# A fused attention and mixture-of-experts kernel: softmax sums folded over the partitions by a chain of accumulating DMAs

## The reference, cut to what matters

```python
q = (c_q @ w_up_q.T).reshape(b, s, H, DH).transpose(0, 2, 1, 3)
k = (c_kv @ w_up_k.T).reshape(b, s, H, DH).transpose(0, 2, 1, 3)
v = (c_kv @ w_up_v.T).reshape(b, s, H, DH).transpose(0, 2, 1, 3)
q = _apply_rope_subspace(q, DR)
k = _apply_rope_subspace(k, DR)
scores = jnp.einsum('bhqd,bhkd->bhqk', q, k) * scale
attn = jax.nn.softmax(scores, axis=-1)
out = jnp.einsum('bhqk,bhkd->bhqd', attn, v)
```

## Time and profile before

| | |
|---|---|
| median of 3 runs | 3598.4 us (3596.11 to 3598.8) |
| the profiled execution | 3596.49 us, its span 3594.9 us |
| busy share of the span | PE 99%, DVE 85%, ACT 76%, POOL 35% |
| mean granted clock | 0.998 |
| DMA queues, share of 16 engines' span | POOL's 46.5% (406.73 MB), SP's 36.2% (383.30 MB) |
| granted clock and DMA share, 300 to 2500 us | 1.00, 0.90 |

### The profile page before, as it was taken

The page is one execution under the profiler, slowest core; times in us unless marked ns, Lnnn a source line. Parts: engine busy times, 40 slices in busy tenths (PEclk is TensorE's granted clock), DMA queues, the critical chain, the costliest instruction groups (busy, mean ns, idle before and its releaser), DMA issues. The chain is left out here.

```text
span 3594.9 us, 79981 instructions
## 1 busy us (share of the span) xinstructions
PE 3542.5 (99%) x24458; PEld 2368.6 (66%) x24458; DVE 3041.8 (85%) x4214; ACT 2741.8 (76%) x3888; POOL 1275.9 (35%) x1304
## 2 busy tenths in 40 slices
PE   6999999999999999999999999999999999999999
PEld 5755555555555555555555555554799999999999
DVE  8878888888888888888888888888777777777799
ACT  5778888888888888888888888888666666666665
POOL 2213232222232323232323232332566666666400
PEclk9999999999999999999999999999999999999999
DMA  7987989898989898989898989896666665666797
GB/s 261 360 295 172 216 194 215 193 216 193 215 195 215 194 215 195 214 196 213 197 211 199 211 199 209 200 210 142 227 213 223 211 226 211 223 212 227 238 370 272
DMA packets 541990, 790.89 MB, mean 220 GB/s; under 512 B 253725, under 2 KB 401310, under 8 KB 505824
## 3 DMA queue, kind: packets, MB, share of 16 engines
q0 software_dynamic: 101648, 406.73, 46.5%
q1 hardware_dynamic: 440272, 383.30, 36.2%
HBM read 453.60 MB, written 138.81 MB: 165 GB/s over the span
## 5 line engine op out<-in xcount | busy, mean ns | idle before, releaser
L1238 ACT ACTIVATE at_ex<-at_st 128x1024 f32<-128x1024 f32 x1024 | 1048.0, 1024 | 217.7 <-PE at_st L1377 214.2
L1435 PE MATMUL at_pv<-at_ex,at_v 128*64 128x512 f32 x4096 | 991.6, 605 | 0.0
L1081 DVE TENSOR_REDUCE at_mx<-at_fr 128x1 fp32r<-128x512 f32 x1024 | 704.3, 688 | 298.6 <-PE at_fr L1445 273.3
L1262 ACT ACTIVATE at_fr<-at_fr 128x512 f32<-128x512 f32 x1024 | 605.4, 591 | 124.7 <-PE at_fr L1445 105.4
L1435 PEld LDWEIGHTS at_pv<-at_ex,at_v 128*64 128x64 f32 x4096 | 248.2, 136 | 504.4 <-issue 504.4
L1377 PE MATMUL at_st<-at_qh,at_kh 64*128 64x512 f32 x2048 | 500.4, 391 | 1.8 <-DMA at_top<-at_mx 1.6
L1377 PE MATMUL at_st<-at_qh,at_kl 64*128 64x512 f32 x2048 | 499.9, 390 | 0.0
L1377 PE MATMUL at_st<-at_ql,at_kh 64*128 64x512 f32 x2048 | 498.5, 389 | 0.0
L1442 PEld LDWEIGHTS at_fr<-at_kdif,at_qh 64*128 64x128 f32 x1024 | 187.9, 183 | 417.3 <-issue 310.6
L1445 PE MATMUL at_fr<-at_kfar,at_qh 64*128 64x512 f32 x1024 | 455.6, 445 | 5.3 <-DVE at_mx L1081 4.3
L1442 PE MATMUL at_fr<-at_kdif,at_qh 64*128 64x512 f32 x1024 | 454.5, 444 | 1.8 <-DVE at_mx L1081 0.9
(11 more groups left out here) (213 smaller groups left out, 6249.2 us busy)
## 6 DMA issues: line engine op xcount, KB each, us to landing
at_cq<-scr_c SPq DMA_DIRECT2D x62, 1024.0 KB, 6.8
at_ck<-scr_c SPq DMA_DIRECT2D x62, 1024.0 KB, 5.7
at_sum<-at_ex POOLq DMA_DIRECT2D x95, 512.0 KB, 5.9
at_sum<-at_sum POOLq DMA_DIRECT2D x95, 512.0 KB, 6.1
scr_v<-pj_v SPq DMA_DIRECT2D x64, 512.0 KB, 6.9
at_v<-scr_v SPq DMA_DIRECT2D x64, 512.0 KB, 7.4
mid_rec<-scr_rec SPq DMA_DIRECT2D x256, 128.0 KB
scr_o<-mid_oT SPq DMA_DIRECT2D x64, 512.0 KB
```

Source lines behind the costliest of these rows:

```text
L1081: e.reduce_max(mx[k // QB][:, h * QB + k % QB:h * QB + k % QB + 1], fr[h][:, :], AX.X).then_inc(s_tr[h], 1)
L1238: e.activation(ex[k][:, :, :], st[u % 2][:, :, :], ACT.Exp, scale=SCALE).then_inc(s_exp, 1)
L1262: e.activation(fr[h][:, :], fr[h][:, :], ACT.Relu).then_inc(s_pos[h], 1)
L1435: mm = e.matmul(pv[n][rows[h], :], v[i.u][:, kt, rows[h]], ex[kt][:, h, :], start=(kt == 0), stop=(kt == KT - 1))
```

## The change

Four things, all in attention:

- DVE adds key tile 3 itself (six additions a half instead of five); `add_sent` is gone.
- In the steady bodies the sum over the partitions is made by DMAs. A tile `total[u]` (128 partitions, 8 KB each) holds the sums of the first half of pair `i` and of the second half of pair `i - 1`. Seven accumulating DMAs (`fold_sums(i, k)`, k = 0 to 6) add the upper half of the rows to the lower half: 64 rows, then 32, 16, 8, 4, 2, 1. Each waits for the landing of the one before. Folds 0 and 1 are issued at the end of body `i`, folds 2 to 6 in body `i + 1`. `spread` then reads row 0 of `total`. The last two pairs are still summed by PE.
- With this the reciprocal moves from step 7 to step 5, the broadcast loads `each` move, and the first addition of a half, which overwrites `total`, waits for the landing of a `spread` (`s_denc`): that of the same body for the second half, that of the body before for the first half.
- `load_c` is issued for one pair in eight, when a new batch starts. SP's loop has eight bodies a turn for that.

```diff
-        NADD = KT - 3
-        SENT = KT // 2 - 1
-        ADDED = (1, 1, 2, None, 3, 3, 4, 5)
+        NADD = KT - 2
+        ADDED = (1, 1, 2, 3, 4, 4, 5, 6)
+        FOLDS = 7
...
+        def joined(j, n):
+
+            return total[j.u if n == 0 else 1 - j.u][:, n, :, :]
...
                 load_w(j, x)
-                load_c(j, x)
+                if j.off % HP == 0:
+                    load_c(j, x)
+                else:
+                    e.sem_inc(s_ld[x][j.u], 16)
...
+            def spread(i):
+
+                wait_apart(e, s_recc, i.n(1, -1), s_apart_s)
+                wait_apart(e, s_fold_sum, i.n(16 * FOLDS), s_apart_s)
+                for n in (0, 1) if prior(i) else (0,):
+                    for h in range(2):
+                        e.dma_start(denc[:, h, n, :], total[1 - i.u][0:1, n, h, :].rearrange("o (p k) -> o p k", p=P)).then_inc(s_denc, 16)
...
             def add_sums(i, n):
 
-                e.wait_ge(s_one[n], i.n(32, 16))
                 wait_apart(e, s_sum, i.n(2 * NADD, NADD * (n + 1)), s_apart)
-                e.dma_start(sums[n][0][i.u][:, :, :], sums[n][1][i.u][:, :, :], accum_op=ALU.add).then_inc(s_one[n], 16)
+                e.dma_start(joined(i, n), late_sum[n][:, :, :], accum_op=ALU.add).then_inc(s_one[n], 16)
+
+            def fold_sums(i, k):
+
+                half = P >> (k + 1)
+                if k:
+                    wait_apart(e, s_fold_sum, i.n(16 * FOLDS, 16 * k), s_apart)
+                else:
+                    wait(e, s_one[1], i.n(16))
+                    wait_apart(e, s_one[0], i.n(16, 16), s_apart)
+                ns = slice(0, NH2) if prior(i.next(1)) else slice(0, 1)
+                e.dma_start(total[i.u][0:half, ns, :, :], total[i.u][half:2 * half, ns, :, :], accum_op=ALU.add).then_inc(s_fold_sum, 16)
...
-                acc = sums[n][a][i.u][:, :, :]
+                acc = late_sum[n][:, :, :] if a else joined(i, n)
                 if not first:
                     e.wait_ge(s_sum, i.n(2 * NADD, NADD * n + ADDED[k] - 1))
                 elif a == 0:
-                    wait(e, s_df, i.n(1, n - 1))
+                    wait(e, s_denc, i.n(64, 64 * n - 96))
...
+                    if g == 5 and prev:
+                        recip(i, slice(0, 2 if prior(i) else 1))
...
-                    if g == 7 and prev:
-                        recip(prev)
...
-                    if g == 4 and prev:
-                        for n in range(NH2):
-                            e.wait_ge(s_one[n], prev.n(32, 32))
-                        if ahead >= 2:
-                            e.wait_ge(s_raw[K], two.n(2, 2))
-                        else:
-                            e.wait_ge(s_osb, i.n(2, 0))
-                        denominators(prev)
+                    if g == 2 and ahead < 2:
+                        e.wait_ge(s_osb, i.n(2, 0))
+                        denominators(i)
```

More of the change, by code:

```diff
@@ L733, in attend_parts @@
         PASSES = ((0, 0), (0, 1), (1, 0))
-        NADD = KT - 3
-        SENT = KT // 2 - 1
-        ADDED = (1, 1, 2, None, 3, 3, 4, 5)
-        c, cos, sin, raw, sums = (below[n] for n in ("c", "cos", "sin", "raw", "sums"))
+        NADD = KT - 2
+        ADDED = (1, 1, 2, 3, 4, 4, 5, 6)
+        FOLDS = 7
+        c, cos, sin, raw, late_sum = (below[n] for n in ("c", "cos", "sin", "raw", "late"))
         swp = [sb(f"swp{x}", [P, S]) for x in "qk"]
@@ L754, in attend_parts @@
         zeros = sb("zeros", [P, 2 * NTOK * D // (NPAIR * P)])
-        sums[0][0] = [sums[0][0][0], sb("sum00_odd", [P, 2, HALF])]
+        sb("above", [P, 368])
+        total = [below["total"], sb("total1", [P, NH2, 2, HALF])]
         ones, osb, den, denc, recc, rec, oT = (bridge[n] for n in ("ones", "osb", "den", "denc", "recc", "rec", "oT"))
@@ L813, in run, with run_batches @@
                     i = At(it, off)
+                    body(i, i.next(-1), 4)
+            for n in range(NPAIR - 5, NPAIR):
+                i = At(0, n)
+                body(i, i.next(-1), NPAIR - 1 - n)
+            tail(At(0, NPAIR - 1))
+        def run_batches(e, prologue, body, tail):
+            prologue()
+            for n in range(3):
+                i = At(0, n)
+                body(i, i.next(-1) if n else None, 4)
+            with e.Fori(0, NBATCH - 1) as it:
+                for off in range(3, 3 + HP):
+                    i = At(it * (HP // 2), off)
                     body(i, i.next(-1), 4)
@@ L909, in body @@
                 one = i.next(1)
-                older = prev and not (isinstance(i.n(), int) and i.n() < 2)
                 if ahead >= 3:
@@ L914, in body @@
                 max_row(i, 6, 0)
-                if older:
-                    each(prev.next(-1), 0)
                 max_row(i, 6, 1)
@@ L919, in body @@
                 max_row(i, 7, 1)
-                if older:
-                    each(prev.next(-1), 1)
                 if ahead:
@@ L930, in body @@
                     max_row(one, 1, 1)
+                if prev and ahead >= 2:
+                    spread(i)
+                elif prev:
+                    spread_rows(i, (0, 1), 0, 2 - ahead)
+                if ahead:
                     max_row(one, 2, 0)
+                    max_row(one, 2, 1)
+                    max_row(one, 3, 0)
                 if prev:
-                    spread(prev, (0, 1))
+                    gather(i, (0, 1) if prior(i) else (0,))
                 if ahead:
-                    max_row(one, 2, 1)
-                    for k in (3, 4):
-                        for h in range(2):
-                            max_row(one, k, h)
+                    max_row(one, 3, 1)
+                    max_row(one, 4, 0)
+                if prev:
+                    if prior(i):
+                        each(i, 1)
+                    each(i, 0)
+                if ahead:
+                    max_row(one, 4, 1)
                     max_row(one, 5, 0)
-                if prev:
-                    if older:
-                        store(prev.next(-1))
-                    gather(prev, (0, 1))
+                if prev and prior(i):
+                    store(prev.next(-1))
             def tail(i):
-                for n in range(NH2):
-                    each(i.next(-1), n)
-                spread(i, (0,))
-                store(i.next(-1))
-                gather(i, (0,))
-                broadcast(i, (0,))
-                spread(i, (1,), 1)
-                gather(i, (1,), 1)
-                broadcast(i, (1,), 1)
+                end = i.next(1)
+                spread_rows(end, (0, 1), 0, 3)
+                gather(end)
+                each(end, 1)
+                each(end, 0)
+                store(i.next(-1))
+                spread_rows(i.next(2), (1,), 1, 4)
+                gather(i.next(2), (1,))
+                each(i.next(2), 1, 32 * NPAIR)
                 store(i)
@@ L1208, in tail @@
                     add_keys(i, n, k)
-                for n in range(NH2):
-                    normalise(i.next(-1), n)
-                recip(i, slice(0, 1))
+                normalise(i.next(-1), 0)
+                recip(i.next(1))
             run(e, prologue, body, tail)
@@ L2329, in build @@
                 "raw": [asb(f"raw{x}", [P, S]) for x in "qk"],
-                "sums": [[[asb(f"sum{n}{a}", [P, 2, HALF])] * 2 for a in range(2)] for n in range(NH2)],
+                "late": [asb(f"late{n}", [P, 2, HALF]) for n in range(NH2)],
+                "total": asb("total0", [P, NH2, 2, HALF]),
             }
```

142 lines of the change are left out of this document (72 added, 70 removed).

## The result

The changed kernel takes 4344.98 us (median of 4 runs, 4339.88 to 4347.51) against 3598.6 us before: 1.2072 times as long, with an interval of 1.2057 to 1.2088. I had predicted 3761.5 us. "Slower" came true, but the loss is 746 us where I had 165, and the time is far outside the range.

A forecast was written before the change was run, and what follows sets the result against it. PE's chain with the denominators and DVE's without them were taken as equally long in step 4. Other terms counted 0; a late fold chain cost 2.7 us a pair, 165 us: 3596.5 + 165 = 3761.5 us, range 3590 to 3920.

The forecast's parts named there:

- Denominators off PE: Step 4 on PE: 1.0 us x 61 leaves PE, but DVE's maximum still holds it; 0 to 7 us gained, taken as 0.
- two chains in step 4: Step 4 of a pair: PE's chain with the denominators and DVE's without them are equally long, 4.90 us between fr matmuls.
- Two more additions: DVE in steps 2 and 6: about 1.13 us each, covered by idle time, taken as 0; uncovered, 2.3 us a pair.
- compressed inputs: Attention's loads: 62 + 62 of 1 MB become 7 + 7; nobody is shown waiting for them, so 0.
- The place of the wait: Step 5 on DVE: the second half's first addition waits on `s_denc`, needed at 1027.47 us, 2.9 us late.
- Steps 1 to 4 of the chain: POOL: `add_sums(prev, 1)` lands at 1012.8, fold 3 at 1013.5, fold 4 issues at 1014.1, fold 6 lands at 1024.0.
- Step 5: Chain's end, SP's `spread`: last issue 2.7 us after the first, landing 3.6 us later, at 1030.4.
- the queries' swaps: POOL: `add_swapped(Q)` waits for fold 6's issue, until about 1022; its result is used in the next body, so 0.
- my high corner: Fold chain and `spread`: links of 4.8 us and a spread landing of 4.8 give 7.8 us a pair, 476 us.
- The second late wait: Rival: DVE also waits about 1 us before the second half's normalisation, 3.7 us a pair, 3822 us; chance 0.17.

## Why the prediction was wrong

**Denominators off PE: right.** I had two chains in step 4, and 0 to 7 us. Without the matmuls 5 us were measured (ratio 0.9986), with DVE's chain shortened as well 29 us (0.9919). In the changed kernel PE waits 0.67 us there.

**Two more additions, compressed inputs: right, with one exception.** 0 was measured for each alone. In the changed kernel a batch's 1 MB load falls beside a fold, once in eight pairs: POOL's links in such a pair, fold 5 to fold 6,

```profile
1639.13 0.77 POOL L1012 DMA_DIRECT2D at_total<-at_total  x1 [3.64 <-DMA at_total<-at_total]
1645.81 0.80 POOL L1012 DMA_DIRECT2D at_total<-at_total  x1 [5.91 <-DMA at_total<-at_total]
```

are 6.7 us, where they are 3.5 otherwise, just behind the issue of that load at 1639.26. It costs 3.2 us in eight pairs, 0.4 a pair.

**The place of the wait: right.** The wait on `s_denc` in step 5 is the one that ends last. I had DVE ready 20.6 us after `add_sums(prev, 1)`; it was 20.7 (1600.28 - 1579.55).

**Steps 1 to 4 of the chain: nearly right.** To fold 4 7.3 predicted, 7.5 measured; then 3.5 and 3.5 predicted, 4.4 and 3.5 measured; to `spread` 3.0 and 2.6. In all 0.8 us too little. POOL's waits for its own small scatters were a good measure for a small accumulate. Of the 9.25 us that DVE waits, the links have this 0.8.

**Step 5 failed.** I had 6.3 us from `spread`'s first issue to the addition, 2.7 of issuing and 3.6 of landing. It took 11.9, 3.0 of issuing and 9.0 of landing. The 3.6 came from a stretch at the end where nothing else moves. In its new place `spread` stands beside the rotation's accumulates and `add_sums(i, 0)`, and I said of them "as before". They were not: in the old place `spread` landed in 4.4 us at the median and 5.4 at the most, in the run without the 1 MB loads. I had worked out myself that the queries' swaps now wait for fold 6's issue, and costed it at 0, since their result is needed only in the next body. What such a neighbour costs is the landing of the DMA that is issued next. 5.6 us a pair, 342 us. How much of it is the nearer traffic and how much the new source was not tried apart; with the swaps cut down, 4.5 of it went away. Even my high corner (4.8 of landing) was from the quiet stretch.

**A term was missing: the clock.** Nothing in the prediction asks what happens to PE's speed when PE waits: 2.7 us in the pair shown, 2.6 on the mean, some 160 us, as much as my whole forecast of the loss.

The sum, per pair: 2.7 predicted, + 0.8 links, + 5.6 `spread`, + 2.7 clock, + 0.4 load = 12.2 us. Times 61 this is 744 us, where 746 were measured. All but the load are read in one pair, so it is luck in part that it comes out within 2 us. The means hold the same: 9.67 us of idle time and 2.60 of slow stretch a pair are 748 us.

**The second late wait** did not come in the changed kernel, where the slow stretch behind the first wait hides it; with the late folds out, DVE waited 2.6 us there. As a mechanism it was right. That the first wait would grow and cover it I didn't see.

## What to carry to other kernels

A landing time belongs to the traffic around it. When a change moves a small DMA into a new place, cost it by rows of that place, and count what the same change holds back and releases there. A wait that stops PE for microseconds can cost twice: add the price of the granted clock to the price of the wait, read from a stretch at the lower level. And before taking work off the busiest engine, look whether a second one has a chain of the same length in that step; if so, little is gained until both are shortened (5 us of 61 here).

## What was not expected of the hardware

- The granted clock fell to 0.50 within one wait of 8.7 us, in the steady pairs, and was back at 1.00 some 6 us after PE had work again. With 16 matmuls more it fell after an idle time of 3.15 us too, with a smaller loss (1.7 us instead of 2.7), and stayed at 1.00 through one of 1.64.
- The accumulate of 512 KB that had taken 6.0 us at the median took 9.9 in the changed kernel, with less traffic in all (115 GB/s from 500 to 2300 us, where it was 205), and 5.9 in the run with the late folds out:

```profile
at_total<-at_late POOLq DMA_DIRECT2D x126, 512.0 KB, 9.9
```

- Four DMAs of 2 KB each, in 16-byte pieces, took 11.9 us from first issue to last landing; in 64-byte pieces 8.3; with the accumulates beside them cut down 7.4 (medians of the pairs). The Trainium skill (DMA: Bandwidth & Descriptors, Rules for kernel authors) advises to join many small transfers into a large one. No run here joins transfers; that larger pieces within a transfer help is shown by the 8.3 us alone.
